# One selective-scan block and one transformer block on a single core: the output phase's attention norm, convolution and feed-forward put in another order

## The reference

```python
y = _ln(y, out_norm_w, out_norm_b) * _silu(z)
attn = jnp.einsum('bhwd,cd->bhwc', y, out_proj_w)
x = shortcut * skip_scale + attn
xl = _ln(x, ln2_w, ln2_b).transpose(0, 3, 1, 2)
hcab = lax.conv_general_dilated(xl, cab1_w, (1, 1), 'SAME', ...) + cab1_b      # 96 -> 32 channels, 3x3
hcab = jax.nn.gelu(hcab, approximate=False)
hcab = lax.conv_general_dilated(hcab, cab2_w, (1, 1), 'SAME', ...) + cab2_b    # 32 -> 96 channels, 3x3
p = hcab.mean((2, 3))
a = jax.nn.relu(p @ ca1_w.T + ca1_b)
a = jax.nn.sigmoid(a @ ca2_w.T + ca2_b)
x = x * skip_scale2 + (hcab * a).transpose(0, 2, 3, 1)
# layer 1, on tokens
t = t + _L1_attn_ref(_ln_t(t), ...)     # 6 heads, no softmax: q (k^T v)
t = t + _L1_ffn_ref(_ln_t(t), ...)      # 96 -> 384 -> 96, operands rounded to 5+2 bit floats, relu between
```

## Time and profile before

| | |
|---|---|
| median of 3 runs (lowest to highest) | 12431.7 us (12424.07 to 12436.66) |
| the profiled execution, and its span | 12431.3 us, 12429.5 us |
| PE / DVE / ACT / POOL busy, share of the span | 70% / 89% / 63% / 78% |
| the same in the 222 us of the third item | 183.5 / 111.2 / 115.2 / 38.4 us |
| TensorE's granted clock, whole span | 0.784 |

### The profile page before, as it was taken

One profiled execution on the slowest core, in us unless ns is written; L12 is line 12 of the kernel. 1 busy time (PEld: TensorE's weight loads), 2 busy tenths in 40 slices (PEclk: granted clock), 3 DMA queues, 4 the chain that ended last, 5 costly groups with the idle time before them and its releaser, 6 DMA issues. The chain is left out here.

```text
span 12429.5 us, 118414 instructions
## 1 busy us (share of the span) xinstructions
PE 8718.8 (70%) x25368; PEld 2449.2 (20%) x25368; DVE 11020.4 (89%) x7214; ACT 7823.5 (63%) x11780; POOL 9754.4 (78%) x4212
## 2 busy tenths in 40 slices
PE   8866666666666666666666666666666666588887
PEld 2321111111111111111111111111111111223222
DVE  6769999999999999999999999999999999554544
ACT  6756666666666666666666666666666666355555
POOL 0039999999999999999999999999999999112120
PEclk9977777777777777777777777777777777788888
DMA  3368888888888878888888888878888887433341
GB/s 105 109 159 183 183 183 180 182 183 183 180 181 181 182 179 183 183 183 180 183 183 183 180 182 181 181 179 183 183 183 183 185 184 157 103 96 84 80 101 28
DMA packets 569246, 2013.70 MB, mean 162 GB/s; under 512 B 82134, under 2 KB 87030, under 8 KB 553974
## 3 DMA queue, kind: packets, MB, share of 16 engines
q1 hardware_dynamic: 568566, 2006.60, 70.8%
HBM read 1599.46 MB, written 406.85 MB: 161 GB/s over the span
## 5 line engine op out<-in xcount | busy, mean ns | idle before, releaser
L845 POOL TENSOR_TENSOR dBu<-rep,BC 128x1024 f32<-128x1024 f32 x3072 | 7152.8, 2356 | 841.5 <-DMA rep<-dd_dram 835.1
L628 PE MATMUL py<-hC,fold 128*32 128x512 f32 x12288 | 2955.9, 860 | 2479.6 <-POOL hC L852 1935.1
L805 DVE TENSOR_TENSOR_SCAN pd<-pd,dBu 128x1024 f32<-128x1024 f32 x2048 | 4670.8, 2281 | 15.9 <-POOL dBu L845 6.6
L676 ACT ACTIVATE pd<-rep,a_now 128x1024 f32<-128x1024 f32 x3072 | 3419.9, 1113 | 930.1 <-DVE hC L813 742.8
L813 DVE TENSOR_TENSOR hC<-pd,BC 128x1024 f32<-128x1024 f32 x2048 | 2507.4, 1224 | 159.9 <-DVE pd L805 26.3
L852 POOL TENSOR_TENSOR hC<-h,BC 128x1024 f32<-128x1024 f32 x1024 | 2403.1, 2347 | 251.7 <-DVE h L805 249.4
L805 DVE TENSOR_TENSOR_SCAN h<-pd,dBu 128x1024 f32<-128x1024 f32 x1024 | 2333.5, 2279 | 24.3 <-ACT pd L676 24.3
L688 ACT ACTIVATE carry<-pd 128x1 f32<-128x1 f32 x1536 | 262.0, 171 | 2080.5 <-DVE hC L813 2063.6
L628 PEld LDWEIGHTS py<-hC,fold 128*32 128x32 f32 x12288 | 521.6, 138 | 4685.7 <-POOL hC L852 2727.1
L1449 POOL TENSOR_TENSOR p_y<-p_y 96x1024 f32<-96x1024 f32 x56 | 134.4, 2431 | 1152.8 <-DMA p_y<-y_dram 1152.8
L597 PE MATMUL pp<-xdbl,w_dt 38*96 38x512 f32 x1024 | 690.5, 807 | 369.3 <-ACT xdbl L705 366.8
(11 more groups left out here) (151 smaller groups left out, 8583.2 us busy)
## 6 DMA issues: line engine op xcount, KB each, us to landing
rep<-dd_dram SPq DMA_DIRECT2D x1024, 768.0 KB, 12.2
BC<-bc_dram SPq DMA_DIRECT2D x2048, 256.0 KB, 9.2
u<-u_dram SPq DMA_DIRECT2D x128, 768.0 KB, 5.4
dd_dram<-LG SPq DMA_DIRECT2D x256, 384.0 KB, 5.2
dd_dram<-RL SPq DMA_DIRECT2D x256, 384.0 KB, 3.5
y_dram<-y SPq DMA_DIRECT2D x256, 384.0 KB, 11.9
p_y<-y_dram SPq DMA_DIRECT2D x61, 1536.0 KB, 15.8
u_dram<-p_u SPq DMA_DIRECT2D x32, 1536.0 KB, 7.6
```

The costliest lines, as they stand in the source:

```text
L628: last = mm(py[32 * g:32 * g + 32, t2(t)], fold[:, :], hC[:, j % 2 * 3 + g, t2(t)], start=(j % 4 == 0), stop=(j % 4 == 3), skip_group_chec ...
L676: go(pd[:, i % 2, :], rep[:, half, 0, g, :], ACT.Exp, scale=a_now[:, i:i + 1]).then_inc(S.exped, 1)
L805: v.tensor_tensor_scan(turned(dst, k), turned(pd[:, i % 2, :], k), turned(dBu[:, i % 4, :], k), 0.0, ALU.mult, ALU.add).then_inc(S.scanned, 1)
L845: nc.gpsimd.tensor_tensor(dBu[:, i % 4, :], rep[:, half, 1, g, :], BC[:, s, 0, r, :], ALU.mult).then_inc(S.dbu, 1)
```

## The change

All of it is in `phase_outputs`:

1. The first nine products-by-four of the first convolution (`grow(0, ...)`) are issued in pieces between the last steps of the drain: two taps ahead of `center_x(6)`, two behind it, two behind `center_x(7)`, three behind `var_x(7)`. The second group follows at once.
2. GELU: one ScalarE instruction on all 128 partitions of a group, from bank 0 or 1 into bank 4 or 5; from there VectorE copies the strips of shifts 0 and 1 (16 copies of 32 partitions); ScalarE makes the strips of shift 2 itself, by GELU from the first bank (8 instructions). The second convolution waits for both (`strip_act`, `strip_dve`).
3. The sigmoid becomes an exponential on ScalarE, an addition of 1 and a reciprocal on VectorE; the logarithm-and-exponential table is loaded behind the last strip.
4. Attention norm: three banks (0, 1, 7) for the centred tile in place of two; centring runs one tile further ahead, transpose and sum one tile later.
5. Feed-forward: `attend` runs two tiles ahead, the square one; bias, ReLU and the output sum come one step earlier, the rounding into `XQ` stands at the head of the step. `turn_y(b + 1, 1, g)` is moved behind the second `attend` sum, two of the eight there and six in the first four steps.

The diff, cut to its core:

```diff
+                def grow(g, taps):
+                    for tap in taps:
+                        for j in range(4):
+                            row = (4 * g + j) * WS + tap // 3
+                            last = mm(ps[32 * j:32 * j + 32, g, :], cab1[:, tap, :],
+                                      XL[:, row:row + WS, tap % 3:tap % 3 + W],
+                                      start=(tap == 0), stop=(tap == 8), skip_group_check=True)
+                    if tap == 8:
+                        last.then_inc(S.cab1_done, 1)
...
+                    if i == NT:
+                        pe.wait_ge(S.xl_made, done(b * NT + 5))
+                        grow(0, range(0, 2))
                     if 2 <= i <= NT + 1:
                         center_x(i - 2)
...
+                grow(0, range(6, 9))
+                pe.wait_ge(S.xl_made, done(b * NT + NT))
+                grow(1, range(9))
 
                 for t in range(NT):
                     n = b * NT + t
-                    pe.wait_ge(S.gelu_made, done(b * 24 + 3 * min(NT, t + 2)))
+                    pe.wait_ge(S.strip_act, done(b * NT + min(NT, t + 2)))
+                    pe.wait_ge(S.strip_dve, done(b * NT + min(NT, t + 2)))
...
                 def center_t(t):
                     n = b * NT + t
                     pe.wait_ge(S.x2_made, done(n + 1))
-                    pe.wait_ge(S.t_normed, done(n - 1))
-                    mm(ps[0:C, t % 2, :], center[:, :], X[:, tile(t)], start=True, stop=True) \
+                    pe.wait_ge(S.t_normed, done(n - 2))
+                    mm(ps[0:C, t_bank[t % 3], :], center[:, :], X[:, tile(t)], start=True, stop=True) \
...
                 attend(0)
+                attend(1)
+                center_f(0)
                 for i in range(NT + 2):
                     if i < NT:
-                        center_f(i)
+                        var_f(i)
+                    if i + 2 < NT:
+                        attend(i + 2)
+                    if i + 1 < NT:
+                        center_f(i + 1)
                     if 1 <= i <= NT:
                         up(i - 1)
-                    if i + 1 < NT:
-                        attend(i + 1)
-                    if i < NT:
-                        var_f(i)
                     if i >= 2:
                         down(i - 2)
...
+                for g in range(2):
                     act.wait_ge(S.cab1_done, done(b * 2 + g + 1))
...
+                    go(ps[:, 4 + g, :], ps[:, g, :], ACT.Gelu, bias=cab1_b[:, :]).then_inc(S.gelu_made, 1)
+                    for j in range(4):
+                        dst, src = strip(4 * g + j, 2, 0)
+                        go(dst, src, ACT.Gelu, bias=cab1_b[32 * j:32 * j + 32, :]).then_inc(S.strip_act, 1)
+                nc.scalar.preload_act_table_set("natural_log_exp_and_others")
...
-                go(att[:, :], ps[0:C, 4, 1:2], ACT.Sigmoid, bias=ca2_b[:, :]).then_inc(S.se_made, 1)
-                nc.scalar.preload_act_table_set("natural_log_exp_and_others")
+                go(att[:, :], ps[0:C, 4, 1:2], ACT.Exp, scale=-1.0, bias=ca2_neg[:, :]).then_inc(S.att_exp, 1)
...
+                for g in range(2):
+                    dve.wait_ge(S.gelu_made, done(b * 2 + g + 1))
+                    for t in range(4 * g, 4 * g + 4):
+                        for dx in range(2):
+                            dst, src = strip(t, dx, 4)
+                            last = v.tensor_copy(dst, src)
+                        last.then_inc(S.strip_dve, 1)
...
+                v.tensor_scalar(att[:, :], att[:, :], 1.0, None, ALU.add).then_inc(S.att_sum, 1)
+                dve.wait_ge(S.att_sum, done(b + 1))
+                v.reciprocal(att[:, :], att[:, :]).then_inc(S.att_made, 1)
...
+                attentiosum(1)
+                if more:
+                    for g in range(2):
+                        turn_y(b + 1, 1, g)
```

More of the change, by code:

```diff
@@ L1393, in body @@
                                                ALU.mult, ALU.add).then_inc(S.x2_made, 1)
[L1394 to L1396 removed]
+                    if i >= 2:
+                        dve.wait_ge(S.t_rstd, done(n - 1))
+                        v.tensor_tensor(TN[0:C, tile(i - 2)], ps[0:C, t_bank[(i - 2) % 3], :], RS1[:, i % 2, :],
                                         ALU.mult).then_inc(S.t_normed, 1)
[L1398 to L1400 removed]
                 dve.wait_ge(S.small_pe, done(b * 4 + 2))
```

139 lines of the change are left out of this document (70 added, 69 removed).

## The result

| | before | after |
|---|---|---|
| median (lowest to highest) | 12429.44 us (12424.07 to 12436.66, 4 runs) | 12216.27 us (12209.33 to 12229.25, 4 runs) |
| ratio, 95% interval | | 0.9829 [0.9812, 0.9846] |

The change takes 213 us; the prediction said 12196, 20 us lower, and its range held the time. The page of the changed kernel shows that the gain lies where the change is: the clock's first 34 slices read as in the earlier trace rows, and the last six, the output phase, stand at 6, 9, 8, 8, 9, 8.

A forecast was written before the change was run, and what follows sets the result against it. No engine was full; the chain from tile to tile and stage to stage bound the output phase. The third item's 31.0 us gain, less 1.6, times 8 is 235: 12431.3 - 235 = 12196 us, range 12140 to 12300.

The forecast's parts named there:

- last affine step ends: End of the drain: delay by two taps (1.7 us) and a clock staying up about cancel; +71.4 for +72.4.
- first convolution ends: Nine second-group taps, 7.7 us, follow the affine step: +79.1 for +87.1, gain 8.0, bounds 4 to 9.
- second convolution ends: Eight tiles at about 2.6 us plus one stop of 0.5: +100.4 for +114.6, gain 14.2.
- factor used: Channel attention: a table load of 1.28 goes, small instructions are added, gain 0.4; +103.3 for +118.0.
- Norm: Attention norm, TensorE-bound: 23.8 us, plus 6 for 12 us at lower clock, plus 1 beside GpSimd: 30.8 for 41.3.
- Both chains: Ahead of the first rounding: the norm's chain reaches +147.5, the scan sums with two turn_y +146.3, within 1.2 us.
- Feed-forward: First rounding to next item, VectorE the next bound: 10 + 10.8 + 13.2 + tail 9.3 = 43.3 for 50.2, gain 6.9.
- the last one of the sum: From third item to mean item: 31.0 us gain less 1.6 gives 29.4, times 8 items is 235 us.
- The clock that stays low for the whole norm: Rival: norm at half clock throughout, 36.8 us, feed-forward keeps 50.2; gain 129, 12302 us; chance 0.28.
- the slower case: Rival: lower clock spreads from the drain over the whole item, 28 us more an item, 12655 us; chance 0.03.
- The copies' contention: Rival: VectorE's 16 copies contend with GpSimd, 2.4 us each, pushing turn_y and scan sums; 12363 us; chance 0.02.
- The second rival: Clock stays up, norm 24.8, GpSimd's scan sums bind: VectorE waits some 7 us before first rounding; 12172 us; chance 0.10.

The follow-up runs named there:

- e4_behind: The changed kernel with all nine taps of the first convolution's first group put back behind the drain's last variance product; 12264.41 us.
- e5_twice: The changed kernel with each of VectorE's 16 strip copies made twice, the second behind a wait for the first; 12234.27 us.
- e2_norm: The kernel before with only the attention norm's new order and its three banks; 12361.5 us, ratio 0.995.
- e7_fill: The changed kernel plus unread products in TensorE's pauses: two of 512 columns ahead of the norm, six of 256 around the four small products; 12164.18 us.
- e11_fill_drain: e9_fill_late plus unread products in the drain: 256 columns at passes 6 and 7, 512 ahead of center_x(7); 12152.31 us.
- e10_fill_before: The kernel before plus the same eight unread products as e7_fill, nothing of the change; 12391.23 us.
- e9_fill_late: e7_fill with the second half's eight turn_y spread over the first five feed-forward steps, none ahead of the first rounding; 12172.0 us.

## Why the prediction was right

The mechanism came as forecast: the shorter stages, the order of what binds, and a time inside the range. The size is too large by 22 us, for a reason in the step from one item to eight. Two readings of the earlier trace rows were off and change little: the slices at 8 are five and not seven, and the 1762 us begin 4 us ahead of the phase's first product. By its own steps, third item, from its first product:

| step | predicted | measured |
|---|---|---|
| last affine step ends | +71.4 | +72.6 |
| first convolution ends | +79.1 | +80.6 |
| second convolution ends | +100.4 | +101.9 |
| factor used | +103.3 | +104.7 |
| Gram sum copied | +134.1 | +133.9 |
| first rounding | +147.5 | +148.2 |
| next item | +190.8 | +189.7 |

Within this item it is late by 1.5 us in the drain and 0.9 ahead of the rounding, early by 1.6 in the norm and 1.8 in the feed-forward. That 1.1 is left of them is in part luck.

**Convolutions.** The sizes came out: 21.3 us for the second one, as predicted; copies of 0.70 for 0.69; one stop of 0.32 for 0.5; a portion of copies that ends at +87.0, ahead of GpSimd's sum. (5.39 / 2 is 2.7 and not the 2.6 of the sum, but the measured 21.3 less its stop is 2.62 a tile, so the 2.6 was good.) The miss is at the front: the affine step was put at +71.4, 1.0 earlier than before, and comes at +72.6. With the taps ahead of it and the clock up it ends at +72.4 to +72.6; with no taps ahead of it and the clock lost on the way (e4_behind) at +71.6 at the earliest. So the two do not cancel: the taps cost 0.8 to 1.0 us more than the clock gives back, and the clock does not always stay up. The first convolution gains 5.9 us in the mean item for the 8.0 of the sum, inside its bounds of 4 to 9; e4_behind measures 6.6 in the profile and 6 in the time.

**Norm.** 30.8 predicted, 29.2 measured here, 29.6 in the mean, and the terms erred against each other. The step of 2.77 at the full clock is what the sum of starts gave. The time at the lower clock was 12 us in my sum. This is the first 24 us of the stage, in the kernel before and then after:

```profile
11230.20:11254.20 24.00, 20.39 (x46) 8.77 (x46) 9.65 (x9) 10.29 (x16) 14.44 (x7) 0.50 0.36 81
```

```profile
11161.80:11185.80 24.00, 21.75 (x83) 10.48 (x84) 13.11 (x15) 15.35 (x26) 10.67 (x4) 0.86 0.73 164
```

0.86 over 24 us is 24 x 0.14 / 0.5 = 6.7 us at the lower level, so 3.4 us of loss for my 6; of the 29.2, 23.8 + 3.4 leave 2.0 for VectorE's products beside GpSimd's additions (1.5 to 2.0 us each there, 0.69 to 0.74 without), where I had 1. e5_twice bears that out: its fourth item's additions start 9 us later, only one of those products takes over 1 us, and the norm takes 27.4 us for the changed kernel's 29.3, with the same stretch at the lower clock. The Trainium skill (TensorE: Matmul & The Clock Gate, What's actually happening) says that activity releases the clock, and in this order the trace agrees in kind: it was back at 1.00 some 10 us after the stage began, even with the old pause in front (e2_norm). The old order, busy for 19.2 of 21 us at 0.50, does not bear it out. What of the two orders makes the difference no run isolates.

**To the rounding.** Both chains met, as predicted: the two `turn_y` end at +145.5 and the rounding is at +148.2, released by ScalarE. That the scan sums are next was shown by e5_twice and e7_fill.

**Feed-forward.** 43.3 predicted, 41.5 measured, 42.8 in the mean. Steps of 5.1 us with a `turn_y` and 4.1 without, VectorE idle for no more than 0.2 us in each: the new bound was named rightly and its steps were a little dear in the sum, 10.8 for 10.2 and 13.2 for 12.0. The old step of 5.34 that they were priced from held a wait of 0.15 us for ScalarE that is gone, and the last of them, without an attended sum, takes 3.6.

**The step that was mis-sized is the last one of the sum.** The third item gained 221.8 - 189.7 = 32.1 us, more than the 31.0 predicted. I turned that into a mean by taking off 1.6, by which the mean item before was the shorter (2.1, if the phase is counted from its first product), and had 29.4 an item. The phase gained (12429.5 - 10671.57) - (12213.1 - 10668.46) = 213.3, 26.7 an item: 5.4 should have come off. Of the seven items that another follows this was the slowest before (its norm was the longest, 41.3 us for 39.0) and is the fastest after: the second and fourth lose 4.2 us in their drain (as does the eighth), the first and seventh have a norm of over 32 us, and the fifth and sixth a feed-forward of over 43. 29.4 - 26.7 = 2.7, times 8, is 22 us, the error of the forecast. By the means of the table the terms that fell short are the first convolution (5.9 for 8.0), the feed-forward (5.4 for 6.9) and the norm (9.4 for 10.5).

**The rivals.** The clock that stays low for the whole norm is out (0.86; 29.6 us); its 36.8 us paid for 24 us at the lower level, less than the whole stage. So is the slower case: it needed some 60 us more of an item at the lower clock, and the third item has some 40 less (34 for 75); the longest stretch that is left is the feed-forward's start, about 14 us. The copies' contention is out as a price (0.70 beside GpSimd) and shown as a chain (e5_twice). The second rival was not this kernel's case. Its chain is e7_fill's, but that its 12172 is near the 12164 there is in part luck: the norm took 28 to 29 us and not 24.8, and VectorE waited 2.3 us for the scan sums and not 7.

## What to carry over

Take an item's stages from several items before making a mean of one, above all where the clock decides: the item chosen here was the slowest before and the fastest after. Where a stage begins behind a pause of TensorE, look at the clock of the first stretch after it; a few products that nobody reads, put into the pause, were worth 43 us here for six of 256 columns. And a wait taken out of one engine's loop turns into the next one's: after these, VectorE's own work in the feed-forward is what is left.

## What the runs showed of the hardware

- Unread products in pauses keep the granted clock at 1.00 in most items through stretches that read 0.50 to 0.65 without them: the feed-forward's start in six of e7_fill's eight items, the drain in all eight of e11_fill_drain's. In the old order's norm they do not (e10_fill_before, six of eight items). They cost no time that the table shows.
- The clock falls in the drain in eight of eight items when all taps stand behind it, and in fewer, none to six, when six taps stand in its waits.
- Items with the same instructions do not lose the clock alike: in the changed kernel's drains the second, fourth and eighth do, in e9_fill_late's, which is the same drain, the first, second and fifth. The stretch ahead of it is equally busy (4.47 of 6 us) where the clock falls and where it stays.
- VectorE's copy of 32 x 504 or 512 numbers from PSUM to SBUF takes 0.70 us from start to start, beside GpSimd and without it (0.71 in e5_twice); its product with both tiles in SBUF takes 0.69 to 0.74 alone and up to 2.8 beside GpSimd's additions (2.77 in e7_fill's row), and GpSimd's four additions 10.7 for 9.3.
- An instruction of VectorE on 96 numbers takes 0.15 us, ScalarE's on the same 0.26.
